# Row attention after group norm: scores issued two rows at a time, the cast of P first on GpSimd, loads of two rows

## The reference, cut to what matters

```python
def _L0_conv_ref(x, W_qkv, b_qkv):            # x: (16, 64, 256, 128)
    scale = C ** 0.5                          # C = 128, two heads of c = 64
    qkv = jnp.einsum('bglc,dc->bgld', x, W_qkv) + b_qkv
    qkv = qkv.reshape(B, G, L, 3, H, c).transpose(3, 0, 1, 4, 2, 5)
    q, k, v = (qkv[0], qkv[1], qkv[2])
    score = jnp.einsum('bghlc,bghmc->bghlm', q, k) / scale
    score = jax.nn.softmax(score, axis=-1)
    out = jnp.einsum('bghlm,bghmc->bghlc', score, v)
    return out.transpose(0, 1, 3, 2, 4).reshape(B, G, L, C)

# _gn: group norm over rows, tokens and the 4 channels of each of 32 groups
x = x + _L0_conv_ref(_gn(x), W_qkv, b_qkv)    # all float32
```

## Time and profile before

| | us |
|---|---|
| median of 3 runs | 4220.36 |
| lowest and highest | 4219.55, 4224.01 |
| the profiled execution, its own time | 4225.53 |
| its span in the trace | 4223.5 |
| busy TensorE matmul / weight load | 3958.7 / 2923.8 |
| busy VectorE, ScalarE, GpSimd | 3759.4, 3125.2, 2134.7 |
| DMA traffic | 809.81 MB, mean 192 GB/s |

### The profile page before, as it was taken

The page is one execution under the profiler, slowest core; times in us unless marked ns, Lnnn a source line. Parts: engine busy times, 40 slices in busy tenths (PEclk is TensorE's granted clock), DMA queues, the critical chain, the costliest instruction groups (busy, mean ns, idle before and its releaser), DMA issues.

```text
span 4223.5 us, 147348 instructions
## 1 busy us (share of the span) xinstructions
PE 3958.7 (94%) x44133; PEld 2923.8 (69%) x44133; DVE 3759.4 (89%) x7138; ACT 3125.2 (74%) x8193; POOL 2134.7 (51%) x3089
## 2 busy tenths in 40 slices
PE   4999999899999999999999899999999999999998
PEld 3767777677776777767777677776767777677776
DVE  6998989889898898988989889898898989989887
ACT  3777777677776777767777677776777777777776
POOL 1555555455554555545555455554555555555554
PEclk9999999999999999999999999999999999999999
DMA  7999898998998989989899998989989998997878
GB/s 197 198 193 201 196 198 196 191 188 199 195 199 181 193 199 198 198 179 200 194 199 198 180 199 197 197 198 181 197 195 201 196 197 193 197 192 166 165 164 167
DMA packets 2438095, 809.81 MB, mean 192 GB/s; under 512 B 2175232, under 2 KB 2437760, under 8 KB 2437760
## 3 DMA queue, kind: packets, MB, share of 16 engines
q1 hardware_dynamic: 2311040, 679.97, 79.7%
q10 hardware_dynamic: 126720, 125.84, 10.7%
HBM read 134.42 MB, written 134.22 MB: 64 GB/s over the span
## 4 chain that ended last, share of the span: by engine, by line
issue 41%; POOL 26%; DVE 15%; POOLq 5%; PE 5%; DVEq 4%; ACT 2%; DMA 1%; SPq 0%; ACTq 0%
POOL p_hi L600 21%; DVE o_norm L455 9%; POOL x_ring L607 4%; POOLq L156 2%; DVEq L460 1%; PE o_bank L315 1%; DVE neg_max L429 1%; POOL y_ring L616 1%; ACT prob L394 1%; PE qk_bank L277 1%; DVE p_lo L436 1%; PE s_bank L299 1%; DVE v_lo L442 1%; POOLq L616 1%; POOLq L607 1%
## 5 line engine op out<-in xcount | busy, mean ns | idle before, releaser
L616 POOL TENSOR_TENSOR y_ring<-image,o_norm 128x256 f32<-128x256 f32 x1024 | 744.5, 727 | 2015.7 <-DVE o_norm L455 2009.9
L394 ACT ACTIVATE prob<-s_bank,neg_max 128x256 f32<-128x256 f32 x4096 | 1604.4, 481 | 189.8 <-issue 177.2
L375 ACT ACTIVATE qk<-qk_bank,b_in 128x256 f32<-128x256 f32 x2048 | 861.0, 472 | 757.2 <-PE qk_bank L277 755.6
L436 DVE SCALAR_TENSOR_TENSOR p_lo<-prob,p_hi 128x1024 f16<-128x1024 f32 x1024 | 1254.3, 1225 | 174.9 <-POOL p_hi L600 144.6
L429 DVE TENSOR_REDUCE neg_max<-s_bank 128x2 f32<-128x512 f32 x2048 | 1309.7, 681 | 35.8 <-PE s_bank L299 35.8
L299 PE MATMUL s_bank<-qk 64*128 64x256 f32 x8192 | 1172.1, 404 | 30.9 <-issue 30.0
L277 PE MATMUL qk_bank<-xc,w_norm 128*128 128x256 f32 x4096 | 1164.2, 407 | 0.0
L600 POOL TENSOR_SCALAR p_hi<-prob 128x1024 f16<-128x1024 f32 x1024 | 1071.4, 1046 | 22.8 <-ACT prob L394 18.1
L277 PEld LDWEIGHTS qk_bank<-xc,w_norm 128*128 128x128 f32 x4096 | 697.1, 190 | 394.9 <-issue 327.0
L299 PEld LDWEIGHTS s_bank<-qk 64*128 64x128 f32 x8192 | 709.4, 187 | 253.2 <-issue 205.3
L315 PE MATMUL o_bank<-v_hi,pt_lo 128*128 128x65 f16 x8192 | 852.9, 193 | 26.6 <-issue 18.0
(11 more groups left out here) (72 smaller groups left out, 2449.4 us busy)
## 6 DMA issues: line engine op xcount, KB each, us to landing
out_dram<-y_ring SPq DMA_DIRECT2D x512, 256.0 KB, 2.5
image<-in_x_dram ACTq DMA_DIRECT2D x240, 512.0 KB, 4.3
pt_hi<-p_hi SPq DMA_TRANSPOSE x1024, 3.3
pt_lo<-p_lo SPq DMA_TRANSPOSE x1024, 3.1
image<-in_x_dram SPq DMA_DIRECT2D x4, 2048.0 KB, 16.2
w_in<-in_L_conv_W_qkv_dram SPq DMA_DIRECT2D x1, 192.0 KB, 2.3
b_in<-in_L_conv_b_qkv_dram SPq DMA_DIRECT2D x3, 0.5 KB, 2.1
```

Source lines behind the costliest of these rows:

```text
L375: ins = act.activation(qk[:, v % 2, t, :], qk_bank[:, t * TOK:(t + 1) * TOK], ACT.Identity, bias=b_in[:, t:t + 1])
L394: ins = act.activation(prob[:, m, c:c + TOK], s_bank[m][h][:, a * TOK:(a + 1) * TOK], ACT.Exp, bias=neg_max[:, m, h, a:a + 1])
L436: dve.scalar_tensor_tensor(out=p_lo[:, v % 2, :], in0=prob[:, v % 2, :], scalar=P_SCALE, in1=p_hi[:, v % 2, :], op0=ALU.mult, op1=ALU.subt ...
L616: pool.tensor_tensor(y_ring[:, m, :], image[:, par, bass.ds(row, 1), :].rearrange("p a c -> p (a c)"), o_norm[:, v % 2, :, :].rearrange("p ...
```

## The change

- TensorE: `scores` runs for rows r and r + 1 in succession in every even step r, and not at all in odd ones. The leads of `project_qk` and `x_transpose` grow by one, and on ScalarE those of `x_copy` and `qk_copy`.
- GpSimd: the list begins with `p_high` of row r (it was the last entry, for row r - 1), then `refill` of row r + 7 (was r + 5), then `finish` of row r - 4.
- VectorE: `p_low` comes first, ahead of `sums`; `v_low` goes ahead of `divide`; the places of the statistics' operations (`next_image`) shift with them.
- SyncE: `store` handles row r - 7 (was r - 6).
- ScalarE's image loads: two rows every second row instead of four rows every fourth. `bring` gets the row's place in the loop body for its wait and its address.
- `X_AHEAD`, which says how far before an image's end its projections begin, is 3 instead of 2.

```diff
@@ -34,13 +34,14 @@
     FINISH = 12
     STATS_FROM = ROWS - FINISH - GROUPS
     assert STATS_FROM % UNROLL == 0 and FINISH % UNROLL == 0
-    X_AHEAD = 2
+    X_AHEAD = 3
     MEASURE = "measure"
     LOADS = 4
     LB = ROWS // LOADS
     SETTLE = UNROLL
     LAG = STATS_FROM
-    CHUNKS = ROWS // UNROLL
+    LOAD_ROWS = 2
+    CHUNKS = ROWS // LOAD_ROWS
     QK, PAIR = HEADS * J * TOK, HEADS * J * J
 
     x_img = x.rearrange("n r (p j) c -> n p r (j c)", j=J)
@@ -176,8 +177,8 @@
                     if what is not None and (place == MEASURE) == (what[0] == MEASURE):
                         share(base, u, par, what, place)
 
-                if coming is not None and u == 0 and bring is not None:
-                    bring(base, *coming)
+                if coming is not None and u % LOAD_ROWS == 0 and bring is not None:
+                    bring(base, u, *coming)
                 order(run, next_image)
 
             def run_image(img, par, first, last):
@@ -188,8 +189,8 @@
                     start = 2 * UNROLL
                     for i in range(-2 * UNROLL, start):
                         if bring is not None and i >= 0:
-                            for c in range(i, CHUNKS - LAG // UNROLL, start):
-                                bring(None, 1, 1, c * UNROLL)
+                            for c in range(i, CHUNKS - LAG // LOAD_ROWS, start):
+                                bring(None, 0, 1, 1, c * LOAD_ROWS)
                         step(i // UNROLL * UNROLL, i // UNROLL * UNROLL, i % UNROLL, par, None, None,
                              (1, 1, ROWS - LAG + i) if i >= 0 else None)
                 else:
@@ -199,12 +200,12 @@
                 with eng.Fori(0, (STATS_FROM - start) // UNROLL) as t:
                     for u in range(UNROLL):
                         step(t * UNROLL + g + start, t * UNROLL + start, u, par, None, None,
-                             None if last else (img + 1, 1 - par, t * UNROLL + (ROWS - LAG + start), first))
+                             None if last else (img + 1, 1 - par, t * UNROLL + (ROWS - LAG + start + u), first))
                 with eng.Fori(0, GROUPS // UNROLL) as t:
                     for u in range(UNROLL):
                         step(t * UNROLL + g + STATS_FROM, t * UNROLL + STATS_FROM, u, par, None,
                              None if last else (MEASURE, img + 1, t * UNROLL + u),
-                             None if final else (img + 2, par, t * UNROLL + (STATS_FROM - LAG)))
+                             None if final else (img + 2, par, t * UNROLL + (STATS_FROM - LAG + u)))
                 for i in range(FINISH):
                     row = ROWS - FINISH + i
                     step(g + row // UNROLL * UNROLL, 0, row % UNROLL, par, row,
@@ -250,7 +251,7 @@
 
             def order(run, next_image):
                 run(-2, transpose_low)
-                run(-6, store)
+                run(-7, store)
                 run(-1, transpose_high)
 
             schedule(sp, order)
@@ -288,7 +289,12 @@
                                    w_norm[:, at[0], 2, :], start=False, stop=(j == J - 1))
                 mm.then_inc(v_done, 1)
 
-            def scores(base, v, at):
+            def scores_of_two(base, v, at):
+                if v % 2 == 0:
+                    scores(base, v)
+                    scores(base, v + 1)
+
+            def scores(base, v):
                 pe.wait_ge(qkc_done, base + (v + 1))
                 if not known_below(base, 2 - v):
                     pe.wait_ge(exp_done, base + (v - 1))
@@ -348,12 +354,12 @@
                     statistics(what[1] * STAT_STEPS, STAT_MM_AT.index(what[2]))
 
             def order(run, next_image):
-                run(0, scores)
-                run(+1, project_qk)
+                run(0, scores_of_two)
+                run(+2, project_qk)
                 run(0, project_v)
                 next_image(0)
                 run(-3, values)
-                run(+3, x_transpose)
+                run(+4, x_transpose)
 
             schedule(pe, order, share)
 
@@ -406,14 +412,14 @@
                 next_image(0)
                 run(-1, exponent, 0)
                 run(-1, exponent, 1)
-                run(+2, x_copy)
-                run(+1, qk_copy)
+                run(+3, x_copy)
+                run(+2, qk_copy)
                 run(0, v_high)
 
-            def bring(base, img, par, row, free=False):
+            def bring(base, u, img, par, row, free=False):
                 if not (free or base is None or known_below(base, LAG)):
-                    act.wait_ge(y_done, base - (LAG - UNROLL))
-                rows = bass.ds(row, UNROLL)
+                    act.wait_ge(y_done, base + (u + LOAD_ROWS - LAG))
+                rows = bass.ds(row, LOAD_ROWS)
                 act.dma_start(image[:, par, rows, :], x_img[img, :, rows, :]).then_inc(loaded[par], 16)
 
             schedule(act, order, share, bring)
@@ -575,13 +581,13 @@
                         dve.wait_ge(stat_step, (what[1] + 1) * STAT_STEPS)
 
             def order(run, next_image):
+                run(-2, p_low)
                 run(-4, sums)
                 next_image(0)
-                run(-2, p_low)
+                run(-1, v_low)
                 next_image(1)
+                run(-4, divide)
                 next_image(2)
-                run(-4, divide)
-                run(-1, v_low)
                 run(0, row_max, 0)
                 run(0, row_max, 1)
                 next_image(3)
@@ -630,9 +636,9 @@
             pool.wait_ge(first_in[0], 16)
 
             def order(run, next_image):
+                run(0, p_high)
+                run(+7, refill)
                 run(-4, finish)
-                run(+5, refill)
-                run(-1, p_high)
 
             schedule(pool, order)
 
```

## The result

| | before | after |
|---|---|---|
| median, us | 4221.4 (4 runs) | 4184.5 (4 runs, 4181.7 to 4187.3) |
| the profiled execution, its own time / span | 4225.5 / 4223.5 | 4181.7 / 4179.7 |
| busy TensorE, VectorE, ScalarE, GpSimd | | 3723, 3832, 2976, 2568 |

A forecast was written before the change was run, and what follows sets the result against it. The prediction took a GpSimd-VectorE ring as the bound, replaced by a ring of two rows' scores through ScalarE's exp. Ring, load issues and statistics summed over images to +189 us: 4415, less 5.2 for the median, 4409; range 4310 to 4510.

The forecast's parts named there:

- The old ring: GpSimd's cast of P and VectorE's division, each started by the other: 3.94 us a row before, claimed to go.
- TensorE's 3.83: TensorE's own work per row in us, 4.04 less 0.21 waiting for v_lo; the row could fall to it.
- The new ring: Chain from one stalled score through qk projection, ScalarE's copy, v_high and exp to the next: 7.75 us for two rows.
- The hand-over: From ScalarE's exp back to TensorE's scores: not shown in the trace, between 0.03 and 0.19 us, taken as 0.15.
- The signs named for it: Expected in the changed profile: scores wait for prob every second row, v_lo's wait nearly gone, pairs near 8.3 and 8.6 us.
- The loads: Image loads issued by ScalarE ahead of exp, inside the new ring: 0.35 us unrolled, 0.55 mid-body, 0.87 at the loop's head.
- +175 us for thirteen images: Full images 1 to 13 at +13.5 us each: +11.5 in 48 looped rows, +2.0 in 16 unrolled rows.
- the sequencer's lead: How far ScalarE's sequencer gets ahead before v_high: at most 0.16 us; 0.10 taken off each load's price.
- the 0.97 there: Price of a load at a loop's head before the lead: 1.24 us from v_high to exp against 0.27.
- the price of the trace of before, 0.45: Load in the unrolled rows of the earlier trace: 0.72 us from v_high to exp against 0.27.
- The first rival: Faster: load issues hidden behind a busy ScalarE, pair 7.75 us, head 0.10, 4140 us in all; chance 0.05.
- the rule weighed there: Instructions wait in the engine's queue while the sequencer reads on, so loads would cost nothing: 4140 against 4409 us.

## Why the prediction was wrong

**The old ring goes: right.** GpSimd's order alone took 103 us off. With both orders the row fell to about 3.7 us, below the "TensorE's 3.83" of the prediction, see below.

**The new ring: right in its edges and its size.** 7.75 us for two rows were forecast; the changed kernel with its loads behind the exps runs 2 x 3.888 = 7.78. The hand-over was taken as 0.15; here exp ends at 43.30 and scores start at 43.35, in the next pair 51.06 and 51.20. The signs named for it came too: scores wait for prob at every second row, v_lo's wait is nearly gone, GpSimd waits for prob (1545 us), the clock stays at 1.00. The pairs alternate near 7.8 and 8.2 us (from cast to cast of the even rows), not 8.3 and 8.6.

**The loads: the step that failed.** The text put three prices on them, 0.35 unrolled, 0.55 in the middle of the body, 0.87 at the head. Measured: 0 and 0 (loads of four rows: no change; pairs of 7.77 us in both places, cast to cast), and about 0.4 at the head (pairs of mostly 8.15 to 8.20 us; 60 us for some 170 heads are 0.35 each). From scores to scores of the odd rows it is the same: in image 7's measuring loop the pair with the load in the middle takes 7.85 us and the one at the head 8.12, and with the loads behind the exps 7.86 and 7.69. With 0, 0 and 0.40, four rows are 2 x 7.77 + 0.40 = 15.94, 3.985 a row, which is the window's 3.98, and nothing of the +175 us for thirteen images is left.

What was mis-sized is the sequencer's lead, "at most 0.16". The even step's v(r-1) was to be ready 5.60 us after scores(r-1), ScalarE free for v_high at 5.76. ScalarE's side was right: 49.15 - 43.35 = 5.80. TensorE's was too long: its v is done at 47.89 + 0.61 = 48.50, 5.15 after the scores. So the lead is 0.65 us. At the head it is 0.57 (v done at 39.77 + 0.61 = 40.38, v_high at 40.95), which takes the 0.97 there down to about 0.4.

What a lead has to cover can be counted from the end of v. The load is issued 0.36 us after it, in the even step (48.50 to 48.86) as in the run with the loads in the odd steps (47.26 to 47.62), and in the latter exp starts 0.85 after it (48.11). In the even step of the changed kernel ScalarE comes to exp 0.65 + 0.26 = 0.91 after the end of v, by itself: the load is hidden, but with 0.06 us to spare. At the head, where the loop's branch and register work stand before the load, it is issued 0.77 after the end of v and exp starts 1.35 after it, against 0.57 + 0.26 = 0.83: the 0.52 seen above. Some 0.08 of it comes back, since the scores follow the start of such an exp by 1.62 us (41.73 to 43.35), and by 1.70 at the same place in the run with the load behind the exps.

The parts of TensorE's side: qk projection to v took 0.96 and 0.86, where I had 1.07 twice, taken from the start-to-start of the scores (6.65 to 7.72 in the earlier trace rows), a different instruction behind a different one; xt to qk took 0.26, where I had the 0.34 of xt to scores. A clean pitch from the qk projection to v was not to be had in the earlier trace rows, where TensorE waits between the two. That wait also made TensorE's own row too long: 4.04 less the 0.21 of the wait was taken as 3.83, and without a wait the row takes 3.66 (1850.40 to 1854.06 above). A pitch across a wait is no pitch, even with the wait taken off.

The load in odd steps shows the same from the other side. There ScalarE is only 0.21 us behind (47.26 to 47.47), and most of the price of the trace of before, 0.45, comes back (0.64 - 0.26 = 0.38 in the row shown). That 0.45 was not a price "without registers", as the prediction had it: the trace has register work of the sequencer ahead of the load of the earlier trace rows too, as the number of the image is the outer loop's.

The first rival named this mechanism ("hidden as in the earlier trace rows"), with a chance of 0.05. The row for it was in the trace: a load issued at 63.46 beside a v_high at 63.83. I let the rows that were nearest in kind, loops and unrolled rows, outweigh the one that was nearest in state, an engine behind its sequencer. The rival's time, 4140, is 45 us below the measured one, mainly as it priced the head at 0.10, and nearly that of the kernel with the load behind the exps, 4124.

Of the rule weighed there (the Trainium skill, "Advanced Engine Details and Errata", section Sequencer Loop: engine instructions wait in the queue while the sequencer reads on), the runs bear out a part. The sequencer does run ahead of a busy engine: in the even step the load is issued 0.29 us before v_high starts (48.86 and 49.15). But it does not issue the load while the input of v_high is not there yet: the issue follows the end of v by 0.36 us in the rows of both steps shown, and in the odd steps it delays exp, which the rule would exclude.

**The sum over images.** The ring and the ordinary rows come out at -1 us an image. Not foreseen at all were the gain at the outer loop's jump (2.5 to 4.2 us, five times) and in the first rows. No run takes them apart.

## What to carry to other kernels

When work is moved into a chain that one engine holds, first add up when each of the other engines is ready at that point: in this kernel the issue of a DMA cost only what the sequencer had not got ahead of its engine, nothing in one step and 0.38 us one step to the side. A pitch is taken from rows without a wait, between the same two kinds of instruction. And a reordering of several engines is worth taking apart: here the new orders of GpSimd and VectorE gave 247 us and the pair of scores took 209 of them back. The parts do not add up, either: alone, GpSimd's order gave 103 us and VectorE's cost 382.

## Not expected of the hardware

GpSimd's add into y_ring took 727 ns before and 1156 in the mean after. In the timeline it is long where VectorE's p_low (41.52 to 42.73) runs beside it and short where it does not:

```profile
2041.58 1.73 POOL L622 TENSOR_TENSOR y_ring<-image,o_norm 128x256 f32<-128x256 f32 x1
...
2044.84 0.73 POOL L622 TENSOR_TENSOR y_ring<-image,o_norm 128x256 f32<-128x256 f32 x1
```

This holds for the whole trace: the 450 adds of 1024 that take 1.40 to 1.82 us all run beside a p_low for at least 0.82 us, and the other 574, none above 0.74 us, for 0.72 at most. In the kernel before, where the add came ahead of the cast, not one ran beside a p_low, and all took 0.72 to 0.74. VectorE's p_low itself went from 1225 to 1326 ns in the mean. Both lie off the ring here. That the two slow each other is read from this coincidence; no run was made to test it.
